# Attention over 1024 tokens: where the fp32 transposes of the probabilities stand on TensorE, and one more tile between their exponential and their use

## What is computed

```python
h = group_norm(x, gn_w, gn_b)                     # 32 groups of 4 channels
hf = h.reshape(Bn, Cn, Hn * Wn)                   # 8 x 128 x 1024
q = jnp.einsum('bcn,oc->bno', hf, wq) + bq
k = jnp.einsum('bcn,oc->bon', hf, wk) + bk[None, :, None]
v = jnp.einsum('bcn,oc->bno', hf, wv) + bv
alpha = jnp.einsum('bnc,bcm->bnm', q, k) / jnp.sqrt(jnp.float32(Cn))
alpha = jax.nn.softmax(alpha, axis=-1)
out = jnp.einsum('bnm,bmc->bnc', alpha, v)
out = jnp.einsum('bnc,oc->bon', out, wo) + bo[None, :, None]
return out.reshape(Bn, Cn, Hn, Wn) + x
```

## Time and profile before

| | us |
|---|---|
| median of 3 runs | 269.64 |
| lowest and highest run | 269.6 and 270.23 |
| span of the profiled execution | 266.8 |
| TensorE products busy | 254.4 (95%) |
| VectorE busy | 220.5 (83%) |
| ScalarE busy | 175.1 (66%) |
| GpSimd busy | 166.3 (62%) |

### The profile page before, as it was taken

The page is one execution under the profiler, slowest core; times in us unless marked ns, Lnnn a source line. Parts: engine busy times, 40 slices in busy tenths (PEclk is TensorE's granted clock), DMA queues, the critical chain, the costliest instruction groups (busy, mean ns, idle before and its releaser), DMA issues.

```text
span 266.8 us, 4984 instructions
## 1 busy us (share of the span) xinstructions
PE 254.4 (95%) x1599; PEld 157.1 (59%) x1599; DVE 220.5 (83%) x403; ACT 175.1 (66%) x338; POOL 166.3 (62%) x182
## 2 busy tenths in 40 slices
PE   2998999999999999999999999999999999999992
PEld 1655565655566655655665566566656556665581
DVE  2779988999888897988889898988979998678752
ACT  2457766766775786667666866766677677667650
POOL 4056394726978189744979089772997359790621
PEclk9999999999999999999999999999999999999999
DMA  4202004110141102320032102320021200211033
GB/s 118 79 0 81 1 0 119 29 53 2 18 143 40 39 2 40 121 79 0 0 93 103 42 0 40 118 79 0 0 79 17 62 0 5 75 39 42 0 82 115
DMA packets 9806, 13.05 MB, mean 49 GB/s; under 512 B 3904, under 2 KB 4672, under 8 KB 9792
## 3 DMA queue, kind: packets, MB, share of 16 engines
q1 hardware_dynamic: 9504, 12.75, 16.8%
q10 hardware_dynamic: 288, 0.13, 0.2%
HBM read 8.65 MB, written 4.23 MB: 48 GB/s over the span
## 4 chain that ended last, share of the span: by engine, by line
PE 90%; DMA 4%; DVE 3%; ACT 1%; issue 1%; ACTq 0%; POOL 0%; DVEq 0%
PE pT L535 21%; PE S L471 10%; PE S L473 10%; PE S L475 10%; PE O L500 10%; PE O L498 10%; PE O L499 10%; PE misc L417 3%; PE misc L416 3%; PE misc L418 3%; DMA wk_sb<-in_L_conv_wk_dram 1%; DMA inv_rows<-inv_line 1%; DMA inv_line<-row_inv 1%; ACT probs L670 1%; DVE pT_lo L828 1%
## 5 line engine op out<-in xcount | busy, mean ns | idle before, releaser
L828 DVE SCALAR_TENSOR_TENSOR pT_lo<-pT,pT_hi 128x512 f16<-128x512 f32 x128 | 82.8, 683 | 22.3 <-ACT pT_hi L682 22.3
L682 ACT ACTIVATE pT_hi<-pT 128x512 f16<-128x512 f32 x128 | 69.9, 596 | 39.8 <-PE pT L535 39.3
L812 DVE TENSOR_REDUCE neg_max<-S 128x1 f32<-128x1024 f32 x64 | 77.7, 1214 | 1.4 <-PE S L475 0.7
L670 ACT ACTIVATE probs<-S,exp_bias 128x1024 f32<-128x1024 f32 x64 | 71.7, 1121 | 1.8 <-DVE exp_bias L818 1.3
L535 PE MATMUL pT<-ident,probs 128*128 128x128 f32 x512 | 67.4, 274 | 1.8 <-DVE pT_lo L828 1.3
L535 PEld LDWEIGHTS pT<-ident,probs 128*128 128x128 f32 x512 | 58.6, 141 | 14.9 <-ACT probs L670 3.6
L498 PE MATMUL O<-pT_hi,v_hi 128*128 128x512 f16 x120 | 45.5, 379 | 0.0
L499 PE MATMUL O<-pT_lo,v_hi 128*128 128x512 f16 x120 | 45.5, 379 | 0.0
L500 PE MATMUL O<-pT_hi,v_lo 128*128 128x512 f16 x120 | 45.5, 379 | 0.0
L327 POOL TENSOR_TENSOR h_hi<-h,zero 128x512 f16<-128x512 f32 x14 | 14.6, 1041 | 47.8 <-DVE h L804 47.8
L471 PE MATMUL S<-h_hi,u_hi 128*128 128x512 f16 x128 | 38.4, 382 | 0.1
(11 more groups left out here) (119 smaller groups left out, 318.9 us busy)
## 6 DMA issues: line engine op xcount, KB each, us to landing
inv_rows<-inv_line SPq DMA_DIRECT2D x16, 256.0 KB, 3.8
out_dram<-y SPq DMA_DIRECT2D x15, 256.0 KB, 2.0
x_sb<-in_x_dram SPq DMA_DIRECT2D x7, 512.0 KB, 3.2
x_sb<-in_x_dram SPq DMA_DIRECT2D x2, 256.0 KB, 3.4
inv_line<-row_inv SPq DMA_DIRECT2D x16, 2.0 KB, 1.4
out_dram<-y SPq DMA_DIRECT2D x2, 128.0 KB, 1.9
wq_sb<-in_L_conv_wq_dram ACTq DMA_DIRECT2D x1, 64.0 KB, 3.4
wk_sb<-in_L_conv_wk_dram ACTq DMA_DIRECT2D x1, 64.0 KB, 3.8
```

The costliest lines, as they stand in the source:

```text
L670: nc.scalar.activation(probs[:, n % 2, :], S[n % 2][:, :], ACT.Exp, bias=exp_bias[:, p, n:n + 1], accum_out=row_sum[:, p, n:n + 1]).then_i ...
L682: nc.scalar.activation(pT_hi[:, g, half * GT:(half + 1) * GT, n % GT, :], pT[half][:, :, :], ACT.Copy, scale=P_SCALE).then_inc(hi_done, 1)
L812: nc.vector.tensor_reduce(out=neg_max[:, p, n:n + 1], in_=S[n % 2][:, :], axis=AX.X, op=ALU.max, negate=True).then_inc(max_step, 1)
L828: nc.vector.scalar_tensor_tensor(out=pT_lo[:, g, ms, n % GT, :], in0=pT[half][:, :, :], scalar=P_SCALE, in1=pT_hi[:, g, ms, n % GT, :], op ...
```

## The change

On TensorE a step j now holds the logits of tile j+1 and the transposes of tile j-1, one tile later than before. The four transposes of half 0 stand singly behind the first four products of the logits, those of half 1 singly behind the first four products of the values. The values run one step later as well (`group_of` counts one more). In the first batch, where no values run yet, and at the end, transposes stand together. There are four buffers of `probs` in place of two.

ScalarE takes in step j high part 0 and high part 1 of tile j-1, then the exponential of j+1. VectorE takes low part 0 of j-1, the maximum and bias of j+1, low part 1 of j-1. Some copies change place: `copy_values` goes to the head of steps 1 and 5, `copy_u` and `copy_v` of steps 0 and 4 to behind high part 1. At the end `last_values(0)` runs behind all transposes; before, it ran on both sides of the last ones.

```diff
+    PB = 4
...
-        probs = sb("probs", [128, 2, N], fp32)
+        probs = sb("probs", [128, PB, N], fp32)
...
-            past = j - GT
+            past = j - GT - 1
...
+            def transpose_one(tile, half, t):
+                b, n, first = tile
+                T = TILES * b + n
+                if t == 0 and half == 0:
+                    pe.wait_ge(exp_done, T + 1)
+                if t == 0 and not first:
+                    pe.wait_ge(lo_done, 2 * T - 1 + half)
+                m = half * GT + t
+                moved = nc.tensor.transpose(pT[half][:, t, :], probs[:, n % PB, m * 128:(m + 1) * 128],
+                                            ident[:, :])
+                if t == GT - 1:
+                    moved.then_inc(tr_done, 1)
...
+                for i in range(6):
+                    c = slice(i % 2 * HALF, (i % 2 + 1) * HALF)
+                    last = nc.tensor.matmul(s[:, c], (q_hi, q_hi, q_lo)[i // 2],
+                                            (h_hi, h_lo, h_hi)[i // 2][:, p, c], start=(i < 2), stop=(i >= 4))
+                    if tile and i < GT:
+                        transpose_one(tile, 0, i)
                 last.then_inc(qk_done, 1)
...
-                for m in (2 * k, 2 * k + 1):
+                for i in range(6):
+                    m = 2 * k + i // 3
                     vh, vl = v_hi[:, pv, m, 0:C], v_lo[:, pv, m, 0:C]
                     ph = pT_hi[:, q, m, :, :].rearrange("p t n -> p (t n)")
                     pl = pT_lo[:, q, m, :, :].rearrange("p t n -> p (t n)")
-                    nc.tensor.matmul(O[:, :], vh, ph, start=(m == 0), stop=False)
-                    nc.tensor.matmul(O[:, :], vh, pl, start=False, stop=False)
-                    last = nc.tensor.matmul(O[:, :], vl, ph, start=False, stop=(m == TILES - 1))
+                    last = nc.tensor.matmul(O[:, :], (vh, vh, vl)[i % 3], (ph, pl, ph)[i % 3],
+                                            start=(m == 0 and i == 0), stop=(m == TILES - 1 and i == 5))
+                    if tile and i < GT:
+                        transpose_one(tile, 1, i)
                 last.then_inc(av_done, 1)
...
-            def transposes(b, n, first):
-                T = TILES * b + n
-                pe.wait_ge(exp_done, T + 1)
-                for half in range(2):
-                    if not first:
-                        pe.wait_ge(lo_done, 2 * T - 1 + half)
-                    for t in range(GT):
-                        m = half * GT + t
-                        last = nc.tensor.transpose(pT[half][:, t, :], probs[:, n % 2, m * 128:(m + 1) * 128],
-                                                   ident[:, :])
-                    last.then_inc(tr_done, 1)
...
+                    tile = (b, j - 1, first and j == 1) if j else (None if first else (b - 1, TILES - 1, False))
+                    hosted = not first or j > GT
                     if j < TILES - 1:
-                        logits(b, p, j + 1, first and j == 0)
+                        logits(b, p, j + 1, first and j == 0, tile if hosted else None)
                     elif not last:
-                        logits(b + 1, np, 0, False)
+                        logits(b + 1, np, 0, False, tile)
+                    else:
+                        for t in range(GT):
+                            transpose_one(tile, 0, t)
+                    if tile and not hosted:
+                        transposes(tile)
...
-                    if not first or j >= GT:
-                        values(b, j, p, first and j == GT)
-                    if last and j == TILES - 1:
-                        last_values(0, (0, 1))
+                    if hosted:
+                        values(b, j, p, first and j == GT + 1, tile)
...
                         else:
                             pe.wait_ge(var_out, b + 2)
                         project_v(b, p, 2)
-                    transposes(b, j, first and j == 0)
-                    if last and j == TILES - 1:
-                        last_values(0, range(2, TILES))
...
-            last_values(1, range(TILES))
+            for t in range(GT):
+                transpose_one((B - 1, TILES - 1, False), 0, t)
+            values(B, 0, 0, False, (B - 1, TILES - 1, False))
+            last_values(0)
+            last_values(1)
...
-                    act.wait_ge(tr_done, 2 * T - 2)
-                nc.scalar.activation(probs[:, n % 2, :], S[n % 2][:, :], ACT.Exp, bias=exp_bias[:, p, n:n + 1],
+                    act.wait_ge(tr_done, 2 * (T - PB) + 2)
+                nc.scalar.activation(probs[:, n % PB, :], S[n % 2][:, :], ACT.Exp, bias=exp_bias[:, p, n:n + 1],
                                      accum_out=row_sum[:, p, n:n + 1]).then_inc(exp_done, 1)
...
-                    if j == 0:
-                        copy_u(b, 1, first)
+                    tile = (b, j - 1, not first) if j else (None if first else (b - 1, TILES - 1, False))
+                    if j == 1 and not first:
+                        copy_values(b - 1, 0, second)
+                    if j == 5 and not first:
+                        copy_values(b - 1, 1, second)
+                    if tile:
+                        high_part(tile, 0)
                     if j == 1:
                         copy_v(b, 1, first)
-                    if j == 3 and not first:
-                        copy_values(b - 1, 1, second)
-                    if j == 4:
-                        copy_v(b, 2, first)
                     if j == 5 and not last:
                         copy_u(b + 1, 0, False)
                     if j == 6 and not last:
                         copy_v(b + 1, 0, False)
-                    if j == 7:
-                        copy_values(b, 0, first)
-                    high_parts(b, p, j, not first)
+                    if tile:
+                        high_part(tile, 1)
+                    if j == 0:
+                        copy_u(b, 1, first)
+                    if j == 4:
+                        copy_v(b, 2, first)
                     if j < TILES - 1:
-                        exponentials(b, p, j + 1, first and j == 0)
+                        exponentials(b, p, j + 1, first and j + 1 < PB)
                         if j == 2 and not last:
                             inverse_deviation(b + 1, 1 - p)
                     elif not last:
...
+            for half in range(2):
+                high_part((B - 1, TILES - 1, False), half)
+            copy_values(B - 1, 0, False)
...
+                    tile = (b, j - 1) if j else (None if first else (b - 1, TILES - 1))
                     if j == 0 and not (first or last):
                         channel_stats(b + 1, 1 - p, turn(r, p, 1))
                         dve.wait_ge(wstep, at(b + 1, 2))
+                    if tile:
+                        low_part(tile, 0)
...
-                    if j == 4 and not last:
-                        normalise(b + 1, 1 - p, 1)
                     if j == 2 and not last:
                         variance_out(b + 1, 1 - p)
                     if j == 3 and not last:
-                        low_parts(b, j, (0,))
                         group_affine(b + 1, 1 - p)
                         normalise(b + 1, 1 - p, 0)
-                        low_parts(b, j, (1,))
-                    else:
-                        low_parts(b, j)
+                    if j == 4 and not last:
+                        normalise(b + 1, 1 - p, 1)
+                    if tile:
+                        low_part(tile, 1)
...
+            for half in range(2):
+                low_part((B - 1, TILES - 1), half)
```

More of the change, by code:

```diff
@@ L445, in project_v, with transposes, logits @@
                 last.then_inc(v_mm, 1)
-            def logits(b, p, n, first):
+            def transpose_one(tile, half, t):
[10 more added lines that the diff above has]
+                    moved.then_inc(tr_done, 1)
+            def transposes(tile):
+                for half in range(2):
+                    for t in range(GT):
+                        transpose_one(tile, half, t)
+            def logits(b, p, n, first, tile=None):
                 T = TILES * b + n
@@ L468, in logits, with values @@
                 s, q_hi, q_lo = S[n % 2], u_hi[:, p, n * 128:(n + 1) * 128], u_lo[:, p, n * 128:(n + 1) * 128]
[L469 to L475 removed]
+                for i in range(6):
[4 more added lines that the diff above has]
+                        transpose_one(tile, 0, i)
                 last.then_inc(qk_done, 1)
[L478 removed]
+            def values(b, j, p, first_group, tile):
                 q, d, g, k = group_of(b, j)
```

50 lines of the change are left out of this document (21 added, 29 removed).

## The result

The changed kernel takes 294.03 us (median of four runs, 293.78 to 294.91), the kernel before 269.62 beside it: a ratio of 1.090, 95% interval 1.087 to 1.093. The forecast was 295.0, between 290 and 301. The profiled execution of the changed kernel spans 293.2 us against 266.8.

What follows compares the result with a forecast made beforehand. TensorE bounds the kernel before; afterwards the 3.89 us ring does. Exponentials 261.8 us against 238.2 (+23.6) and tail +1.8 on the 266.8 span give 292.2; plus 2.8 from span to time, 295.0 us, range 290 to 301.

Steps and rivals of the forecast that it cites:

- A hidden load: Rival on TensorE: weight loads hidden behind products leave 0.054 us per transpose, giving 243 us; chance 0.03.
- The ring: ScalarE and VectorE: high part 0, low part 0, maximum, bias, exponential, next high part 0; 3.89 us per tile; chance 0.87.
- a change of 0: TensorE: a transpose costs 0.109 us wherever it stands, so 512 take 55.8 us before and after.
- idle time in every tile before a transpose whose releaser is a low part: Sign expected in the changed profile on TensorE, with its busy share falling to about 88%.
- The copies of the bank: ScalarE, steps 1 and 5: product-bank copies ahead of high part 0 add 2 x 0.48 us per steady batch.
- The deviation: ScalarE: its logarithm and exponential stand between step 2's exponential and high part 0, adding 0.33 us per batch.
- step 0: VectorE alone, with bias, low part 1, statistics, low part 0 and maximum, takes 4.03 us, 0.14 over the ring.
- the longer bias behind the token term: VectorE, tiles 0, 3 and 6: the bias takes 1.35 us, adding 3 x 0.10 us per batch.
- the step in which v is projected: Steps 3 to 4, way over TensorE and ScalarE's copy of v: 4.60 us between exponentials, 0.71 over the ring.
- Batch 0: First batch: a first step of about 1.7 us, seven of 3.89 and 1.0 of additions, 29.9 us.
- The tail: End of run: last attention half 10.4 us behind the last exponential, 1.8 later than before, the DMA no longer deciding.
- at no cost: Product-bank copies move to steps 1 and 5, making GpSimd's result and store two steps later, without costing time.

Runs made afterwards that it cites:

- the cut: Fewer transposes: first two of each half's four left out from batch 1; kernel before 269.95 to 256.56 us, changed kernel 294.03 to 291.0 us.
- the pad: A 128-column scratch write on VectorE ahead of every maximum: changed kernel 298.08 us (1.102), kernel before 270.77 us (1.003).
- the maximum first: Changed kernel with VectorE taking the maximum of tile j+1 ahead of low part 0 of tile j-1: 286.06 us (1.058).
- the transposes together: Changed kernel with all eight transposes behind the logits: 297.46 us; with the maximum also ahead of low part 0: 273.07 us.
- maximum first and fewer: Changed kernel, maximum ahead of low part 0, first two transposes of each half left out from batch 1: 273.35 us (1.015).

## Why the prediction was right, and where its terms were off

**What bounds before.** That TensorE does is borne out by the cut there, though only for the first 13 us of it: VectorE and GpSimd stand closer behind than "covered" said. One figure was loose: "30.3 at 3.78 per tile" averages in the short first and last batches; a steady batch took 30.8 before.

**Transposes at 0.109 us.** Right in both directions, by the pair of 0.325 us. A hidden load would have shown 0.27. The Trainium skill, page "TensorE: Matmul & The Clock Gate", section "LDWEIGHTS (loading the stationary operand)", gives a load as its columns divided by 1.2, 107 ns for 128. The trace disagrees with the reading that the transpose's own load is its pitch, for with a 512-column product ahead, under which a load has time to run, the transpose still takes 0.109. It could then be the load of the product behind it that takes the 0.109. Against that stand the small products of v, of 129 columns in fp16, each with a load of its own of 128 columns, which follow one another by 0.057:

```profile
102.73 0.22 PE L399 MATMUL misc<-wvc_hi,h_hi 128*128 128x129 f16 x1
102.79 0.22 PE L400 MATMUL misc<-wvc_lo,h_hi 128*128 128x129 f16 x1
```

What a transpose spends its 0.109 on these runs don't show.

**The ring.** Right in each of its five terms (3.90 measured, 3.89 forecast), and borne out by the pad (what is put into it comes out once per tile) and by the kernels with the maximum first. What the forecast didn't see is the second ring: it named the waits that hosted transposes put in front of the maximum, and found them covered. They are, while low part 0 stands ahead of the maximum: it then releases the next transposes before that maximum starts. Behind maximum and bias it comes 1.46 us after that maximum's start (89.24 to 90.70), and the ring of 3.96 closes. So "a change of 0" for the single transposes holds only for TensorE's own time: of the 24.4 us lost, the maximum first recovers 8.0, the transposes together as well another 13 (286.06 to 273.07), and 3.4 stay lost.

One sign that the forecast named didn't come: "idle time in every tile before a transpose whose releaser is a low part". TensorE waits for a low part 16 times in the whole run, 15.7 us in all, of which 2.73 in batch 0 and about 1.5 in each steady batch, at the low part that stands behind affine and normalisation. In between it works off what it is behind: taken start to start, some 31 of the 33.1 us of the second batch are products that follow one another without a wait. The cut of 22 us there gave 3 all the same, since the exponentials wait for the ring and not for TensorE.

**What a batch adds.** A steady batch came to 33.1 outside the rolled loop and 33.9 in it, against 33.6 and 34.1. The copies of the bank add 0.48 to 0.50 to their steps (4.37 to 4.39), where the forecast had 0.48. From the timeline of ScalarE, batch 1, step 5:

```profile
70.51 1.12 ACT L668 ACTIVATE probs<-S,exp_bias 128x1024 f32<-128x1024 f32 x1
...
71.61 0.59 ACT L651 COPY av<-O 128x512 f32<-128x512 f32 x1
72.08 0.62 ACT L680 ACTIVATE pT_hi<-pT 128x512 f16<-128x512 f32 x1
```

The deviation (0.33; that step takes 4.22, 3.89 + 0.33) and step 0 (4.03; 3.96 to 4.17 in the steady batches) held too. Three terms were too large: 0.39 in place of 0.31 from bias to exponential came on four tiles of eight in the rolled loop and not on six; the longer bias behind the token term adds its 0.10 only in the rolled loop, where it measures 1.35, and not outside, where it is 1.25 like the others; and the step in which v is projected was put at 4.60 and took 4.41 outside the loop, 4.50 to 4.58 in it. Its mechanism is there, in batch 2, step 4:

```profile
99.14 1.11 ACT L668 ACTIVATE probs<-S,exp_bias 128x1024 f32<-128x1024 f32 x1 [1.37 <-DVE exp_bias L823]
...
102.87 0.27 DVE L823 TENSOR_SCALAR exp_bias<-neg_max,c_tok 128x1 f32<-128x1 f32 x1
...
103.28 0.38 ACT L642 COPY v<-misc 128x258 f32<-128x258 f32 x1 [0.17 <-PE misc L401]
103.55 1.12 ACT L668 ACTIVATE probs<-S,exp_bias 128x1024 f32<-128x1024 f32 x1
```

The bias is there at 102.87 and would let the exponential start at 103.2; the copy of v, released by TensorE, holds it until 103.55. From the bias of tile 4 (98.83) to this exponential it is 4.72, where the forecast had 4.91. Term by term: affine and half a normalisation took 1.40 (put at 1.50), the hand-over behind the last small product 0.20 (estimated at 0.25), copy to exponential 0.27 from start to start (0.38 was its recorded length); transposes and products took 1.57 (1.52), the six small products 0.35 (estimated at 0.34, right).

**Batch 0, the miss.** Put at 29.9, it took 32.22, and one step of it 6.00 us instead of 3.89. TensorE sat idle there for 2.73 us, waiting for a low part that stood behind affine and normalisation. Before that gap was over, at 32.5 us, the granted clock fell to its lower level (0.50 of full speed, 1.2 GHz), and it stayed there until 39.4. The row of TensorE, then stretches of 2 us (PE, PEld, DVE, ACT, POOL busy and count, granted clock, DMA share, GB/s):

```profile
33.48 1.11 PE L441 MATMUL pT<-ident,probs 128*128 128x128 f32 x4 [2.73 <-DVE pT_lo L833]
```

```profile
30.00:32.00 2.00, 0.63 (x4) 0.42 (x4) 1.88 (x5) 0.56 (x1) 0.00 (x0) 1.00 0.00 0
32.00:34.00 2.00, 0.52 (x3) 0.53 (x4) 1.95 (x5) 1.14 (x3) 1.04 (x1) 0.63 0.01 4
34.00:36.00 2.00, 2.00 (x12) 1.59 (x11) 1.96 (x5) 1.32 (x3) 1.16 (x2) 0.50 0.00 0
36.00:38.00 2.00, 2.00 (x7) 1.07 (x6) 0.51 (x1) 0.92 (x3) 1.92 (x2) 0.50 0.00 0
38.00:40.00 2.00, 2.00 (x8) 0.95 (x7) 1.53 (x2) 0.68 (x2) 1.65 (x4) 0.66 0.00 0
```

For one tile TensorE was the bound at half speed: the exponentials there start at 35.55 and 41.55, 2.1 us above the ring. With 2.1 taken off, batch 0 is 30.1. In the kernel with the cut, whose first batch has the same work, the same gap of 2.73 us was followed by no fall, and its batch 0 took 29.81. What failed here is thus not a term of the ring but one that the sum didn't have: a fall of the granted clock, which came while TensorE was idle. Whether the idle time alone brings it these runs don't show.

**The tail.** Forecast 1.8 longer, with the last attention half 10.4 us behind the last exponential and TensorE its releaser. It starts 10.35 behind (279.40 to 289.75) and waits for TensorE. A second wait wasn't foreseen: from the timeline of the end,

```profile
284.57 0.58 ACT L651 COPY av<-O 128x512 f32<-128x512 f32 x1
...
285.29 1.52 POOL L351 TENSOR_TENSOR attn<-av,inv_rows 128x512 f32<-128x512 f32 x1 [9.40 <-ACT av L651]
...
286.95 1.27 POOL L359 TENSOR_TENSOR y<-attn,xres 128x512 f32<-128x512 f32 x1
...
288.41 0.62 DVE L952 TENSOR_TENSOR attn<-misc,inv_rows 128x256 f32<-128x256 f32 x1 [3.01 <-POOL y L359]
...
289.75 0.60 DVE L952 TENSOR_TENSOR attn<-O,inv_rows 128x256 f32<-128x256 f32 x1 [0.26 <-PE O L528]
```

The first of the last halves waits 3.0 us for GpSimd, which had waited for the late copy of the bank. That the copies of the bank move "at no cost" is wrong here, at the end; it cost little only because TensorE was later still, by 0.26 us.

**The start**, called untouched, is 0.7 us later in this execution. Both kernels start the first logits at about 13.0, with products some 0.42 us apart. Then the third and fourth product, in the timeline of the kernel before,

```profile
13.81 0.66 PE L473 MATMUL S<-h_lo,u_hi 128*128 128x512 f16 x2
```

and in that of the changed kernel:

```profile
13.71 1.06 PE L475 MATMUL S<-h_lo,u_hi 128*128 128x512 f16 x2
```

In the kernel before, the slow pitch ended with these two; here it lasted until 15.4. That isn't the change: in the kernel before with four buffers, with the pad and with the cut, the slow pitch lasts until 14.7 to 16.1 and the first exponential starts at 17.59, 17.34 and 16.93.

**The sum.** 17.34 + 262.06 + 13.8 (last exponential to the end) = 293.2 of span, against a forecast of 292.2: +0.7 start, +2.3 batch 0, -2.1 steady and last batches. That misses of +3.0 and -2.1 nearly cancel is luck.

A second pair cancels in the step from span to time: the profiled span came 1.0 longer than forecast, and the 2.8 that the forecast added to it, seen in one execution of the kernel before, was 1.1 too much. Each execution has its own span on record: for the changed kernel 293.2, 292.3, 292.1 and 292.3, with times 1.7 to 1.8 above. In the kernel before, beside the experiments, the time lies 1.7 to 2.9 above the span, mostly 1.7 to 1.9, and the spans reach from 266.6 to 269.5, so that the profiled 266.8 was a short one. The three executions of the changed kernel that weren't profiled are 0.9 to 1.1 shorter than the profiled one, at a mean granted clock of 0.994 against 0.986; that fits a shorter fall of the clock in them, but where it fell isn't recorded.

## What to carry to other kernels

Before moving work a tile later, write down the ring for each engine order: start to start from each instruction to the one it releases or precedes, back to its own successor in the next tile. If the sum for one tile is above the busiest engine's time, the order is the bound, and neither buffers nor less work elsewhere will help. When one ring is opened, look for the next before counting the gain; a wait that is hosted inside another chain's products ties the two chains together, and two harmless edits can each close a ring with the other. To prove a ring, put a known small cost into it: it comes back once per tile, in a kernel in which the engine that it was given to is idle 27% of the time.

## What was not expected of the hardware

- In a gap of 2.73 us in which TensorE was idle, the granted clock fell, and it was down for 6.8 us. In the profiled executions it fell at about the same place with transposes together (6.8 us), with the pad (3.4, gap 2.81) and with maximum first (3.4, where the gaps are 1.29 and 0.92). It did not with fewer transposes, nor with maximum first and fewer, whose first batches have the same gaps and the same work as those without the cut. What tells them apart these runs don't show.
- The first logits came 0.42 us apart until 13.9 us in one execution and until 15.4 in the other, while the views of the profile give the granted clock as 1.00 from 12 us on in both. The clock entries of these traces begin only at 13.93 and 15.47 us, just where the pitch changes, and a view takes the time ahead of them as 1.00. The pitch is the one that a granted clock of 0.50 gave in batch 0 (0.43), so the engine most likely ran at half clock there.
- From the start of a bias to the start of its exponential it took 0.31 us outside the rolled loop and inside it 0.40 in tiles 0 to 3 and 0.31 in tiles 4, 6 and 7, for the same two instructions.
- A write of 128 columns on VectorE is recorded with 0.165 us and adds 0.088 to the round that it stands in.
- At a granted clock of 0.50 the fp32 transposes came 0.215 us apart (33.74 and 33.96 in the changed kernel), at 1.00 0.109: their pitch follows the clock like that of the products (0.43 and 0.216).
